# Key-value products placed behind the first Gram tile, and the second batch's first chunk loaded into the key weights' place

## What is computed

```python
k = (ctx_1024 @ Wk.T + bk).reshape(B, 1601, 16, 32)
v = (ctx_1024 @ Wv.T + bv).reshape(B, 1601, 16, 32)
kv = jnp.einsum('bthd,bthe->bhde', k, v)
att = jnp.einsum('bqhd,bhde->bqhe', q, kv) * scale
```

## Time and profile before

| | us |
|---|---|
| median of 3 runs | 593.75 |
| lowest and highest | 591.79, 593.78 |
| the profiled execution | 591.89 |
| its span, first to last instruction | 590.1 |
| TensorE busy | 555.5 |
| VectorE, ScalarE, GpSimd busy | 378.6, 282.7, 245.5 |

### The profile page before, as it was taken

One profiled execution on the slowest core, in us unless ns is written; L12 is line 12 of the kernel. 1 busy time (PEld: TensorE's weight loads), 2 busy tenths in 40 slices (PEclk: granted clock), 3 DMA queues, 4 the chain that ended last, 5 costly groups with the idle time before them and its releaser, 6 DMA issues.

```text
span 590.1 us, 11774 instructions
## 1 busy us (share of the span) xinstructions
PE 555.5 (94%) x4875; PEld 474.3 (80%) x4875; DVE 378.6 (64%) x482; ACT 282.7 (48%) x486; POOL 245.5 (42%) x182
## 2 busy tenths in 40 slices
PE   9985879989898998989999999999999999999997
PEld 7874759878696986969767999987878888888886
DVE  5867967396655947567358737757657446876741
ACT  3484495692938839386174263233224113334320
POOL 2398959374775737757502500301434544000000
PEclk9999889999899898998999999999999999999999
DMA  8555241332233123300564001211941321799501
GB/s 303 161 214 197 81 170 72 111 138 89 92 140 105 71 89 98 147 22 2 170 153 171 11 3 64 83 71 30 241 169 72 112 103 72 157 233 246 150 0 72
DMA packets 31414, 69.13 MB, mean 117 GB/s; under 512 B 6928, under 2 KB 6928, under 8 KB 28432
## 3 DMA queue, kind: packets, MB, share of 16 engines
q1 hardware_dynamic: 31376, 68.58, 37.4%
HBM read 67.39 MB, written 1.18 MB: 116 GB/s over the span
## 4 chain that ended last, share of the span: by engine, by line
PE 72%; ACT 10%; issue 5%; DVE 5%; POOL 1%; DVEq 0%; ACTq 0%; POOLq 0%
PE ps L352 14%; PE ps L354 13%; PE ps L353 13%; PE ps L916 8%; ACT kv L606 6%; PE ps L936 3%; PE ps L940 3%; ACT mb L633 2%; PE ps L989 2%; PE ps L927 2%; PE ps L926 2%; DVE par L1521 2%; PE ps L932 2%; PE ps L931 2%; PE ps L1227 1%
## 5 line engine op out<-in xcount | busy, mean ns | idle before, releaser
L508 POOL TENSOR_TENSOR psum_tmp<-psum_tmp,raw 128x512 f32<-128x512 f32 (+1 forms) x88 | 164.8, 1873 | 30.8 <-DVE lo L1473 22.4
L916 PE MATMUL ps<-hi 128*128 128x256 f32 (+1 forms) x384 | 124.1, 325 | 10.2 <-DVE lo L1473 10.2
L606 ACT ACTIVATE kv<-par 32x320 f32<-32x320 f32 x112 | 52.6, 469 | 69.9 <-DVE par L1521 68.5
L916 PEld LDWEIGHTS ps<-hi 128*128 128x128 f32 x384 | 76.0, 198 | 12.0 <-DVE lo L1473 11.0
L1473 DVE TENSOR_TENSOR lo<-raw,hi 128x2048 fp32r<-128x2048 f32 (+1 forms) x29 | 74.1, 2555 | 7.8 <-ACT hi L582 7.5
L352 PE MATMUL ps<-hi,gh 128*128 128x512 f32 x192 | 75.5, 393 | 0.0
L354 PE MATMUL ps<-hi,gl 128*128 128x512 f32 x192 | 74.8, 390 | 0.0
L353 PE MATMUL ps<-lo,gh 128*128 128x512 f32 x192 | 74.7, 389 | 0.0
L561 POOL TENSOR_TENSOR sx<-sx,raw 128x512 f32<-128x512 f32 x32 | 41.1, 1290 | 76.4 <-DVE raw L1863 76.4
L803 ACT ACTIVATE hi<-raw 128x2048 fp32r<-128x2048 f32 x14 | 26.8, 1917 | 89.3 <-PE ps L354 80.5
L352 PE MATMUL ps<-wvh,gh 128*128 128x512 f32 x128 | 51.0, 398 | 0.8 <-ACT mb L633 0.8
(11 more groups left out here) (227 smaller groups left out, 1186.7 us busy)
## 6 DMA issues: line engine op xcount, KB each, us to landing
raw<-in_ctx SPq DMA_DIRECT2D x23, 1024.0 KB, 4.9
raw<-in_ve SPq DMA_DIRECT2D x8, 1024.0 KB, 6.7
raw<-in_oe SPq DMA_DIRECT2D x8, 1024.0 KB, 6.1
wk<-gm_rows SPq DMA_DIRECT2D x8, 512.0 KB, 8.9
g<-gm_rows SPq DMA_DIRECT2D x8, 512.0 KB, 10.4
raw<-in_ctx SPq DMA_DIRECT2D x16, 128.0 KB, 4.1
cb<-in_ctx SPq DMA_DIRECT2D x8, 256.0 KB, 3.3
xres<-in_x SPq DMA_DIRECT2D x1, 1024.0 KB, 9.5
```

Of the source, the lines that this page charges most:

```text
L508: pool.tensor_tensor(psum_tmp[0:k, :], (raw[:, 0, :] if t == 1 else psum_tmp[0:k, :]), raw[0:k, t, :], ALU.add).then_inc(ctx_sum, 1)
L606: ins = act.activation(turned[dst, :, :, src], flipped[src, :, dst].rearrange("p (r s) n -> p r s n", s=2), ACT.Copy)
L916: pe.matmul(dst, hi[:, t, cols], x, start=start and opens, stop=t == CH * ROWS - 1 and closes, skip_group_check=True)
```

## The change

It does five things. The key-value products of b - 2 run between the first and second tile of Gram b (in the last Gram too). ScalarE makes the copies of product blocks 2 and 3 before the split of the next batch's second chunk. The first chunk of batch 1 is loaded early, without a wait, into `wk`, from where its split and its row sums read it; the key weights are loaded into `wk` when that chunk's sum is done, ahead of the loads of batch 2, and TensorE waits for them once before the loop. The row sums of batch 0 begin with the second chunk and end with the first, and the loads of batch 1's other chunks follow that order. The order of batch 0 and 1 on ScalarE and VectorE is rewritten to suit.

```diff
+    FIRST_ORDER = [*range(ROWS, NSLOT), *range(ROWS)]
+    FIRST_SUMMED = [NADD, ROWS - 1, 2 * ROWS - 1, 2 * ROWS]
...
+        def in_wk(b, c):
+            return isinstance(b, int) and b == 1 and c == 0
+        def ctx_rows(b, c):
+            return wk[:, :, :] if in_wk(b, c) else raw[:, chunk(c), :]
...
             sp.dma_start(mb[:, :, :], blocks(a["WqT"])).then_inc(ld_wq, 16)
+            load_ctx(1, 0)
             sp.dma_start(wv_raw, blocks(a["WvT"])).then_inc(ld_wv, 16)
...
-            next_ctx(1, 0)
-            next_ctx(1, 1)
-            sp.dma_start(wk[:, :, :], blocks(a["WkT"])).then_inc(ld_wk, 16)
-            next_ctx(1, 2)
-            next_ctx(1, 3)
+            for c in range(1, CH + 1):
+                sp.wait_ge(ctx_sum, FIRST_SUMMED[c])
+                load_ctx(1, c)
             sp.dma_start(beta, a["beta"].rearrange("(o d) -> o d", o=1).broadcast_to([P, D])).then_inc(ld_beta, 16)
             next_tail(1)
+            sp.wait_ge(ctx_sum, NADD + SUMMED[0])
+            sp.dma_start(wk[:, :, :], blocks(a["WkT"])).then_inc(ld_wk, 16)
             with sp.Fori(2, B) as b:
...
-            sums(0, True)
-            with pool.Fori(1, B) as b:
-                sums(b, False)
+            sums(0, FIRST_ORDER)
+            sums(1, [*range(NSLOT)])
+            with pool.Fori(2, B) as b:
+                sums(b, [*range(NSLOT)])
...
-            turn(0, range(0, 8))
             ctx_high(1, 0, False)
-            turn(0, range(8, 16))
+            turn(0, range(0, 10))
             ctx_high(1, 1, False)
+            turn(0, range(10, 16))
             act.wait_ge(ld_wv, 16)
             act.wait_ge(q_mm, KC)
             act.activation(wvh[:, :, :], wv_raw, ACT.Copy).then_inc(w_hi, 1)
-            lower_blocks(0, range(0, 8))
             ctx_high(1, 2, False)
             ctx_high(1, 3, False)
-            lower_blocks(0, range(8, 16))
+            lower_blocks(0)
...
-                m_copy(b - 1, (2,))
+                m_copy(b - 1, (2, 3))
+            def rest_of(b):
                 ctx_high(b + 1, 1, False)
-                m_copy(b - 1, (3,))
...
-                        if between and t == 2:
+                        if between and t == 1:
                             between()
...
-                    pe.wait_ge(ld_wk, 16)
...
             products_of(0, True)
+            pe.wait_ge(ld_wk, 16)
             with pe.Fori(2, B - 1) as b:
-                kv_part(b - 2)
-                gram(b, False)
+                gram(b, False, lambda: kv_part(b - 2))
                 products_of(b - 1, False)
-            kv_part(B - 3, range(0, 2))
-            gram(B - 1, False, lambda: kv_part(B - 3, range(2, KC)))
+            gram(B - 1, False, lambda: kv_part(B - 3))
...
             query_copy(0)
+            ctx_low(1, 0)
+            query_copy(1)
             with_tail(0, True)
             straight_sums(0)
-            query_copy(1)
-            ctx_low(1, 0)
             query_copy(2)
+            ctx_low(1, 1)
             query_copy(3)
-            ctx_low(1, 1)
+            turned_sums(0)
+            flip_up(0)
             dve.wait_ge(consts, 11 + NE)
             sum_copy(0)
-            turned_sums(0)
-            flip_up(0)
```

More of the change, by code:

```diff
@@ L154, in perceiver_block @@
         ld_ctx = [sem(f"ld_ctx{c}") for c in range(CH + 1)]
-        ld_first, ld_second = sem("ld_first"), sem("ld_second")
+        ld_first, ld_second, ld_early = sem("ld_first"), sem("ld_second"), sem("ld_early")
         first_hi, first_lo = sem("first_hi"), sem("first_lo")
@@ L228, in chunk, with landed @@
             return slice(ROWS * c, ROWS * c + ROWS) if c < CH else slice(CH * ROWS, CH * ROWS + 1)
-        def landed(c):
-            return 16 if c < CH else 32
+        def landed(b, c):
+            if in_wk(b, c):
+                return ld_early, 16
+            if c == 0 and not (isinstance(b, int) and b == 0):
+                return ld_ctx[0], b * 16
+            return (ld_ctx[c], b * 16 + 16) if c < CH else (ld_ctx[c], b * 32 + 32)
+        def in_wk(b, c):
+            return isinstance(b, int) and b == 1 and c == 0
+        def ctx_rows(b, c):
+            return wk[:, :, :] if in_wk(b, c) else raw[:, chunk(c), :]
         def upper(t, bank_step):
@@ L361, in load_ctx @@
                     src = a["ctx_1024"][b, c * P * ROWS:(c + 1) * P * ROWS, :].rearrange("(p r) d -> p r d", r=ROWS)
-                    sp.dma_start(raw[:, chunk(c), :], src).then_inc(ld_ctx[c], 16)
+                    sp.dma_start(ctx_rows(b, c), src).then_inc(ld_early if in_wk(b, c) else ld_ctx[c], 16)
                 else:
@@ L490, in rstd_of, with sums, rows @@
                 pool.tensor_tensor(rstd[:, i:i + 1], vareps[:, i:i + 1], expo[:, 0:1], ALU.pow).then_inc(s_rstd[n], 1)
-            def sums(b, first):
-                n = 0
-                for t in range(1, NSLOT):
+            def sums(b, order):
+                def rows(t):
+                    return wk[:, t, :] if in_wk(b, t // ROWS) else raw[:, t, :]
+                for n, t in enumerate(order[1:]):
                     c, k = (t // ROWS, P) if t < CH * ROWS else (CH, HALF)
-                    if first and t == 1:
+                    if n == 0 or t % ROWS == 0:
+                        pool.wait_ge(*landed(b, c))
+                    if order is FIRST_ORDER and t == 0:
                         pool.wait_ge(ld_first, 16)
                         pool.wait_ge(ld_second, 16)
+                    if n:
+                        pool.wait_ge(ctx_sum, b * NADD + n)
+                    elif order is FIRST_ORDER:
                         pool.wait_ge(wq_low, 1)
[L500 to L504, removed]
+                    else:
                         pool.wait_ge(sum_out, b)
-                    if t in SUMMED:
+                    if t % ROWS == ROWS - 1 or t == NSLOT - 1:
                         pool.wait_ge(ctx_lo, b * 4 + c + 1)
-                    pool.tensor_tensor(psum_tmp[0:k, :], (raw[:, 0, :] if t == 1 else psum_tmp[0:k, :]), raw[0:k, t, :],
+                    pool.tensor_tensor(psum_tmp[0:k, :], psum_tmp[0:k, :] if n else rows(order[0]), rows(t)[0:k, :],
                                        ALU.add).then_inc(ctx_sum, 1)
-                    n += 1
             def masks():
@@ L576, in ctx_high @@
                 r = chunk(c)
-                act.wait_ge(ld_ctx[c], b * landed(c) + landed(c))
+                act.wait_ge(*landed(b, c))
                 if not first:
@@ L581, in ctx_high @@
                     act.activation(lo[0:HALF, r, :], raw[0:HALF, r, :], ACT.Copy, scale=0.5)
-                act.activation(hi[:, r, :], raw[:, r, :], ACT.Copy).then_inc(ctx_hi, 1)
+                act.activation(hi[:, r, :], ctx_rows(b, c), ACT.Copy).then_inc(ctx_hi, 1)
             def first_high(c, t):
@@ L608, in turn, with lower_blocks @@
                     ins.then_inc(turn_done, 1)
[L610 to L614, removed]
+            def lower_blocks(b):
+                act.wait_ge(upflip_done, b * 4 + 4)
+                for n in range(16):
                     src, dst = quarters(n)
                     ins = act.activation(low_pairs(dst)[:, :, :, src], upflip[src, :, :, dst], ACT.Copy)
-                if ns.stop == 16:
-                    ins.then_inc(lower_done, 1)
+                ins.then_inc(lower_done, 1)
             def gh_high(b):
@@ L663, in turn_between_copies @@
                 turn(b, range(10, 16))
-                m_copy(b - 1, (2,))
+                m_copy(b - 1, (2, 3))
+            def rest_of(b):
                 ctx_high(b + 1, 1, False)
-                m_copy(b - 1, (3,))
-            def rest_of(b):
                 ctx_high(b + 1, 2, False)
@@ L1472, in ctx_low @@
                 dve.wait_ge(ctx_hi, b * 4 + c + 1)
-                dve.tensor_tensor(lo[rows, r, :], raw[rows, r, :], hi[rows, r, :].bitcast(F32), ALU.subtract).then_inc(ctx_lo, 1)
+                dve.tensor_tensor(lo[rows, r, :], ctx_rows(b, c)[rows, :, :], hi[rows, r, :].bitcast(F32), ALU.subtract).then_inc(ctx_lo, 1)
             def by_block(t):
```

## The result

The changed kernel takes **568.32 us** (median of 4 executions, 566.83 to 569.16), the kernel before 593.76 beside it on the same chip (4 executions, 591.79 to 594.02). The ratio is 0.9576, with a 95% interval of 0.9547 to 0.9604: 25.4 us less between the medians, where the prediction had worked out 25.4 from the one profiled execution and forecast a median of 567.5. The profiled execution took 568.38 us, its span is 566.7, 23.4 shorter than before. Two single executions in what follows lie far outside the others of their kernel, 625.84 us of the kernel before and 2490.62 us of the one with the chunk of batch 2 early, whose median without it is 560.46 instead of 560.72.

A forecast was written before the change was run, and what follows sets the result against it. TensorE was taken as the bound, busy 555.5 of 590.1 us. Terms 21.6 + 4.7 - 0.6 - 0.3 = 25.4 off 591.89 gave 566.5; about half of 1.86 added gave 567.5, range 560 to 575.

The forecast's parts named there:

- The loop: Second tile of Gram 2 to third tile of Gram 7: 21.6 us gained, 14.6 from five waits, 7.0 from clock.
- The rival by which it would still swing: In the loop, the clock still swings without the waits: 7.0 us less gain, 574.5 us, chance 0.12.
- The dead heat at the second chunk: In loop Grams, VectorE's low part ends at 125.05, TensorE arrives at 125.15; 0.6 us charged, bounds 0 and 6.
- The row sums: At the loop's end they wait for VectorE's copy of the last sum: 0.3 us lost.
- the start: Before the second tile of Gram 2: that tile starts at 84.3 instead of 89.04, 4.7 us gained.
- the adds: GpSimd's three adds of batch 1's row sums, awaited by batch 2's first chunk: 47.5 + 3.2 + 3.2 + 1.3 = 55.2.
- the first key-value wait: TensorE's wait at 84.88 before the first key-value products; nearly all of the start's 4.7 us was put there.
- the start gains too: Rival: batch 2's chunk lands at 58.0, block 2 starts 4.8 earlier, clock holds; 6.2 us more gain, 561.3, chance 0.09.
- The sum: Whole kernel: 21.6 + 4.7 - 0.6 - 0.3 = 25.4 us off the profiled 591.89, giving 566.5.
- the half of 1.86 us: Added to 566.5 because the median before stood 1.86 above the profiled execution, giving 567.5.

The follow-up runs named there:

- The loop alone: Kernel before with only key-value products behind the first Gram tile and copies 2 and 3 ahead of the split: 567.30 us, again 567.37.
- the start alone: Changed kernel with the old loop order back, keeping early chunk, reordered sums and key weights behind them: 590.64 us, ratio 0.9942 to the kernel before.
- the kernel with the sum copy last: On the fastest kernel, flips of batch 1 ahead of batch 2's first low part, and batch 1's sum copy after the flips up: 560.90 us.
- the fastest kernel: Changed kernel with batch 2's first chunk loaded when its place is free, and VectorE's low part, sum copy and small reductions reordered in the start: 558.86 us.

## Why the prediction was right, point by point

**The loop was right to a tenth.** The prediction had 159.8 us from the second tile of Gram 2 to the third tile of Gram 7; after, it is 246.30 - 86.51 = 159.79, 21.6 us less than before. The wait goes because copy 3 is there half a microsecond before TensorE asks for it, and it takes both edits: with either one alone 1.0 or 1.4 us remain. The rounds are 31.6 us, as worked out from the one round before that lost no clock.

**The clock holds.** The rival by which it would still swing (574.5) is refuted: 1.00 over 110 us of the loop. The two kernels with waits of 1.0 and 1.4 us in each round show more, since even with these the clock stays at 1.00. The Trainium skill's page "TensorE: Matmul & The Clock Gate", section "A second HAM failure mode: psum-queue depth-cycling", tells of a kernel in which TensorE idles for very short times between groups of matmuls, so frequently that the clock swings. One such gap a round did not make it swing in these two kernels (1.00 over 130 us), and the changed kernel has no gap in its loop that could test the rule; more frequent gaps were not tried.

**The dead heat at the second chunk cost nothing**, where 0.6 us were charged and 6 feared: after, no Gram of the loop waits for a low part. The row sums lost 0.5 us, not 0.3.

**The step that was mis-sized is the start: 2.5 us instead of 4.7.** Its mechanism is as written: the chunk of batch 2 is late, so flips, copy 0 and product block 2 are late, TensorE stands still and the clock falls. The size went wrong at the adds. I had the third add done at 55.2; it ended at 57.55. The first began 1.9 us later than assumed, of which 0.8 is this execution's whole start (first flips at 28.71, before at 27.95), and the second and third took 4.90 instead of 4.5. Every later mark is late by the same: flips 71.69 for 69.3, block 2 at 76.53 for 74.2, second tile at 86.51 for 84.3. Gram 1 also came later than worked out, at 63.46 for 59.6: its third chunk was ready at 54.77 for 52.4, and the clock fell behind that wait too, for which nothing was charged. This cost nothing, because TensorE then waited for copy 0 in any case, 7.46 us where 9 were forecast.

**The attribution was loose too.** I put the first key-value wait into the start's term, since it lies there in time. The loop alone shows that its edits take that wait with its clock, 4.4 us. The prediction's "4.7 us, nearly all of it the first key-value wait" was thus right about the wait, but the edit that takes it is the loop's, and the new start beside the loop stands at minus 1.0 to 1.3 us. The rival *the start gains too* (561.3) missed for the change but its condition is real: with the chunk of batch 2 early, 560.72 was measured.

**The sum**: 21.6 + 2.5 - 0.5 = 23.6 of the 23.4 us between the two spans. The forecast came nearer than its terms: the sum gave 566.5 for a profiled execution that took 568.38, and the half of 1.86 us that was added on top took away half of that miss. That the medians differ by 25.4, just as worked out, is luck. The profiled execution before lies 1.9 us under its median because it is one that lost less clock: it kept the clock through one whole round and has a mean of 0.977, while of 26 others on record (without the one at 625.84) 22 have 0.971 or 0.974, at 591.25 to 595.72 us.

## What to carry to other kernels

When one change moves several things, price each part alone: here two small edits of the loop carry all of it, and the large rewrite of the start carries nothing until one load is issued at the moment its place is free. An early operand is worth only what the next load in the same queue lets it be worth; follow the chain from each moved load to the engine that waits for it last. And a stall of TensorE is to be priced with the clock that it costs afterwards, which here was a third of the loop's gain; how often it is paid differs from execution to execution, so one profile is not enough to price it.

## What was not expected of the hardware

**Which waits cost clock.** A lone stand of TensorE of 1.0 to 1.4 us, once in each round, took no clock in 130 us of two kernels, and 7.5 us did. In between it goes both ways. The same wait of 2.92 us at the same place was followed by the full clock in the profiled kernel before and by the low level in the start alone (the rows at 120.76 and 119.31); a wait of 1.86 us was followed by 0.54 in the kernel with VectorE's start reordered; and in the kernel with the sum copy last, the wait of 2.07 us was followed by 1.00 and that of 2.10 by 0.51. So the length of the wait alone does not tell, and what does is not shown here. The stretches after the last two:

```profile
93.00:96.00 3.00, 3.00 (x13) 2.48 (x14) 3.00 (x2) 0.00 (x0) 2.92 (x2) 1.00 0.14 60
...
102.00:105.00 3.00, 3.00 (x9) 2.34 (x8) 0.00 (x0) 2.92 (x7) 2.76 (x3) 0.51 0.97 285
```

**The start scatters.** The first flips of batch 0 come behind the first loads and Gram 0. They begin between 27.42 us (the fastest kernel) and 30.84 (the one with the split between the copies), though both kernels do the same up to there. The first matmul of the queries scatters as well, from 26.45 to 29.68 us in the same two. So a start that is 0.8 us later, as in the changed kernel's profile, says nothing of its edits.
